# One gather for keys and values, and a GpSimd that weighs them: the edge attention of a four-layer graph network

## The chip, the cores and the metric

The kernel runs on one core of a Trainium2 chip, as one program. The metric is device time in microseconds, the median of three runs. A core has TensorE (PE; PEld is its weight load), VectorE (DVE), ScalarE (ACT), GpSimd (POOL) and SyncE (SP), which only starts DMAs here. Engines run side by side and wait for one another on semaphores. Arithmetic is fp32 throughout.

## What is computed

Four graph layers and four expert layers follow one another on 3125 nodes of 256 features and 50,000 edges sorted by destination. Only the first graph layer matters here:

```python
enh = node_features + 0.1 * query_emb[None, :]        # node_features = layernorm(x)
Q, K, V = [(enh @ W + b).reshape(N, 4, 64) for W, b in ...]
mod_k = K[src] + 0.2 * rel_w[edge_relations][:, None, :]
scores = einsum('ehd,ehd->eh', Q[dst], mod_k) / 64 ** 0.5
ex = exp(scores - segment_max(scores, dst)[dst])
w = ex / segment_sum(ex, dst)[dst]
agg = segment_sum(w[:, :, None] * V[src], dst)
msgs = where(deg > 0, agg, V)
x = layernorm(msgs.reshape(N, 256) @ Wo + bo + node_features) * gamma + beta
```

## The kernel before

The nodes are 25 tiles of 125 (T, P). The edges are 391 chunks of 128. A chunk can touch two node tiles, so the kernel goes through "visits", pairs of a chunk and a tile; there are 416 (VT), done in 104 batches of four (VB). For each visit `tile_of_visit` holds the tile's number, `src_of_visit` the source nodes of the 128 edges, `rel_dst` their destination within the tile.

The phases run one after another, with a barrier of all engines between them:

- `qkv_phase`: VectorE normalises the rows, TensorE turns and multiplies them. A first loop over the tiles makes the keys, in five groups of five tiles (L474 to L505, L532 to L537); a second loop makes values and queries in turn (L538). SP stores each group of keys to the DRAM table `k_table` and of values to `v_table`, 640 KB each (L454). When all keys are stored, GpSimd starts the gathers of the first eight batches (L464).
- `score_phase`: per batch GpSimd gathers the key rows of 4 x 128 edges, 1 KB each, with four indirect DMAs (L93), into a ring of eight batches. VectorE builds 0/1 matrices ("hits", L688), TensorE turns them and multiplies them with queries and relation weights, ScalarE copies, VectorE adds the key rows (L747), multiplies (L751) and reduces (L753). GpSimd refills a slot when L747 has read it (`freed`).
- `weights_phase`: maximum per node by scans, and the exponential. GpSimd meanwhile gathers the value rows of the first eight batches (L860).
- `attend_phase`: GpSimd gathers value rows like the keys. VectorE multiplies them by the weights into `summand` (L1008), copies the weights beside them (L1011), reads the four tile numbers of the batch before from memory into registers (L79), makes the hits three batches ahead (L688), and adds the four products of the batch before, from PSUM, to their tiles of `sums` or `odd_sums` (L997). TensorE multiplies hits and summands (L1034).
- `message_router_phase`: loads the nodes' own values from `v_table` (L1303) and goes on.

No planner decides an order: each engine's queue is the order of the code.

Of the kernel before, what the change touches and what calls it, by code (L numbers as in the profile page):

```python
# [23 lines left out]
N = 3125  # L24
# [60 lines left out]
def early_gathers(env, pool, table):  # L85

    for k in range(RING):
        start_gather(env, pool, table, k)

def start_gather(env, pool, table, k):
    for i in range(VB):
        pool.indirect_dma_start(env.ring[:, k % RING, i, :], None, table, bass.IndirectOffsetOnAxis(  # L93
            env.src_of_visit[:, k * VB + i:k * VB + i + 1], 0)).then_inc(env.gathered[k % RING], 16)

class Gather:

    def __init__(self, env, ph, table, batches):  # L100
        self.env, self.table, self.batches = env, table, batches
        self.rows = env.ring
        self.freed = ph.sem()
        self.passed = ph.sem()
        self.base = list(env.gathered_base)
        for s in range(RING):
            env.gathered_base[s] += 16 * VB * len(range(s, batches, RING))

    def gpsimd(self, pool):
        for k in range(RING, self.batches):  # L110
            pool.wait_ge(self.freed, k - RING + 1)
            pool.sem_inc(self.passed, 1)
            start_gather(self.env, pool, self.table, k)

    def wait(self, engine, k):

        engine.wait_ge(self.env.gathered[k % RING], self.base[k % RING] + 16 * VB * (k // RING + 1))
# [297 lines left out]
def qkv_phase(env):  # L415
# [6 lines left out]
    with ExitStack() as st:  # L422
# [7 lines left out]
        k_rows = sb(env, st, "k_rows", [P, 2 * GT, D])  # L430
        v_rows = sb(env, st, "v_rows", [P, 2 * GT, D])
        turned_ps = ps(env, st, "turned_ps", [128, 2, 512])
        k_ps = ps(env, st, "k_ps", [128, 2, 512])
        q_ps = ps(env, st, "q_ps", [128, 2, 512])
        v_ps = ps(env, st, "v_ps", [128, 2, 512])
        moments = Moments(env, st, ph, "nodes")
        present, prepared, w_landed, bias_landed, query_landed, query_scaled = [ph.sem() for _ in range(6)]
        normed_made, turned, turned_out, k_multiplied, k_made = [ph.sem() for _ in range(5)]
        q_multiplied, v_multiplied, q_made, v_made = [ph.sem() for _ in range(4)]
        k_stored = [ph.sem() for _ in range(2)]  # L440
        v_stored = [ph.sem() for _ in range(2)]
        with nc.Block() as block:

            @block.sync
            def _(sp):
# [4 lines left out]
                for rows, table, made, stored in ((k_rows, env.k_table, k_made, k_stored), (v_rows, env.v_table, v_made, v_stored)):  # L450
                    for g in range(G):
                        half = g % 2
                        sp.wait_ge(made, (g + 1) * GT)
                        sp.dma_start(table[g * GN:(g + 1) * GN, :].rearrange("(t p) d -> p t d", p=P),  # L454
                                     rows[:, half * GT:(half + 1) * GT, :]).then_inc(stored[half], 16)
                for half in range(2):
                    sp.wait_ge(v_stored[half], 16 * len(range(half, G, 2)))

            @block.gpsimd
            def _(pool):  # L460
                pool.memset(eps[:], 1e-5).then_inc(prepared, 1)
                for half in range(2):
                    pool.wait_ge(k_stored[half], 16 * len(range(half, G, 2)))
                early_gathers(env, pool, env.k_table)  # L464

            @block.vector
            def _(v):
# [8 lines left out]
                def keys(g):  # L476
                    if g >= 2:
                        v.wait_ge(k_stored[g % 2], 16 * (g // 2))
                    for t in group(g):
                        v.wait_ge(k_multiplied, t + 1)  # L480
                        v.tensor_tensor(k_rows[:, t % (2 * GT), :], k_ps[0:P, t % 2, 0:D], bias_bc[:, D:2 * D], ALU.add).then_inc(k_made, 1)

                def values(g):
                    if g >= 2:
                        v.wait_ge(v_stored[g % 2], 16 * (g // 2))
                    for t in group(g):
                        v.wait_ge(v_multiplied, t + 1)
                        v.tensor_tensor(v_rows[:, t % (2 * GT), :], v_ps[0:P, t % 2, 0:D], bias_bc[:, 2 * D:3 * D],
                                        ALU.add).then_inc(v_made, 1)
                        v.wait_ge(q_multiplied, t + 1)  # L490
                        v.tensor_tensor(env.q[:, t, :], q_ps[0:P, t % 2, 0:D], bias_bc[:, 0:D], ALU.add).then_inc(q_made, 1)
# [5 lines left out]
                for i in range(G + 1):  # L497
# [6 lines left out]
                    if i >= 1:  # L504
                        keys(i - 1)  # L505
                v.tensor_copy(env.mean[:], moments.mv[:, :, 0:1].rearrange("p t o -> p (t o)"))
                v.tensor_copy(env.rstd[:], moments.rstd[:])
                for g in range(G):
                    values(g)

            @block.tensor
            def _(pe):
                def product(out, t, part, done):
                    for k in range(K2):
                        mm = pe.matmul(out[0:P, t % 2, 0:D], x_t[:, t, k * P:(k + 1) * P], w_sb[:, k, part * D:(part + 1) * D],
                                       start=k == 0, stop=k == K2 - 1)
                    mm.then_inc(done, 1)

                def key(t):
                    pe.wait_ge(turned_out, t + 1)  # L520
                    if t >= 2:
                        pe.wait_ge(k_made, t - 1)
                    product(k_ps, t, 1, k_multiplied)

                pe.wait_ge(w_landed, 16)
                for t in range(T):
# [7 lines left out]
                    if t % GT > 0:  # L534
                        key(t - 1)
                    if t % GT == GT - 1:
                        key(t)  # L537
                for t in range(T):  # L538
                    if t >= 2:
                        pe.wait_ge(v_made, t - 1)  # L540
                    product(v_ps, t, 2, v_multiplied)
# [2859 lines left out]
```

## Time and profile before

| | |
|---|---|
| median of three runs | 5564.5 us (5561.1 to 5566.32) |
| profiled execution | 5557.42 us |
| its span | 5555.6 us |
| TensorE busy | 4191.8 us (75%) |
| VectorE busy | 2496.2 us (45%) |
| GpSimd busy | 2332.9 us (42%) |
| ScalarE busy | 1159.9 us (21%) |
| gathers of keys, L93 | 416, busy 422.5 us |
| gathers of values, L93 | 416, busy 427.6 us |
| DMA over the span | 95 GB/s on average |

The span is the time from the first to the last instruction; the execution's own time lies 1.8 us above it. Busy shares are averages over phases with different limits. "issue" as the reason of an idle stretch means that the engine waited for nothing that the profile shows, mostly for its own sequencer. Each fp32 product of a visit is two records of TensorE (832 for 416).

### The profile page before, as it was taken

What the parts mean: (1) busy time and instruction counts of PE and PEld (TensorE: products, weight loads), DVE (VectorE), ACT (ScalarE), POOL (GpSimd) and SP (SyncE); (2) the same over time, 40 slices, a digit from 0 to 9 for tenths busy, and PEclk for the clock granted to TensorE, in tenths of its full rate; (3) what the DMA queues carried; (4) which work ended last, traced back from release to release, by engine and by line L of the source; (5) the groups of instructions that cost most, each with busy time, mean ns of one, the idle gap of its engine ahead of it and who ended that gap; (6) DMA issues with size and microseconds to landing.
All of it is one profiled execution on the core that took longest, in us unless ns stands there. A gap on an engine that the chain in (4) does not pass through costs nothing. (4 is left out here: it accounts for less than half of the span.)

```text
span 5555.6 us, 68719 instructions
## 1 busy us (share of the span) xinstructions
PE 4191.8 (75%) x20094; PEld 3185.7 (57%) x20094; DVE 2496.2 (45%) x4951; ACT 1159.9 (21%) x2617; POOL 2332.9 (42%) x2376
## 2 busy tenths in 40 slices
PE   5899935554573777799977899766559999665689
PEld 3666623333562555699976888544437677443445
DVE  4799976666525444265656000322223222222253
ACT  1244400000122000232222444200003333100023
POOL 0677767775245777100000111357760000477710
PEclk9999968776696999899987999667889999888888
DMA  2333323331273333210001999333331000233300
GB/s 74 104 101 100 100 71 100 102 102 56 84 229 123 103 103 104 89 39 7 7 31 52 314 322 324 113 88 103 103 102 35 1 1 10 76 102 103 103 24 14
DMA packets 315546, 530.11 MB, mean 95 GB/s; under 512 B 76398, under 2 KB 226171, under 8 KB 315086
## 3 DMA queue, kind: packets, MB, share of 16 engines
q0 software_dynamic: 106944, 292.17, 18.3%
q1 hardware_dynamic: 208268, 233.65, 12.9%
q8 instruction: 189, 3.10, 0.2%
q14 instruction: 145, 1.19, 0.1%
HBM read 471.59 MB, written 54.05 MB: 95 GB/s over the span
## 5 line engine op out<-in xcount | busy, mean ns | idle before, releaser
L2442 POOL DMA_INDIRECT gathered_rows<-k_table,index x1176 | 1153.4, 981 | 1073.5 <-ACT index L2431 716.1
L2528 PE MATMUL sum_ps<-gathered_rows,hit 128*125 (+1 forms) x3328 | 983.9, 451 | 662.6 <-SPq L2448 431.7
L2528 PEld LDWEIGHTS sum_ps<-gathered_rows,hit 128*125 128x125 f32 (+1 forms) x3328 | 704.6, 221 | 941.5 <-issue 825.1
L93 POOL DMA_INDIRECT rows_all<-k_table,src_of_visit x416 | 422.5, 1016 | 197.0 <-issue 118.2
L93 POOL DMA_INDIRECT rows_all<-v_table,src_of_visit x416 | 427.6, 1028 | 147.9 <-issue 126.1
L1034 PE MATMUL ps_sum<-summand,hit 128*125 128x261 f32 x832 | 294.2, 515 | 245.1 <-DVE summand L1011 216.7
L2512 DVE TENSOR_TENSOR node_sums<-node_sums,sum_ps 125x256 f32 x244 | 102.8, 422 | 771.3 <-PE sum_ps L2528 771.3
L1034 PEld LDWEIGHTS ps_sum<-summand,hit 128*125 128x125 f32 x832 | 198.3, 250 | 340.6 <-issue 299.3
L2431 ACT ACTIVATE index<-src_of_chunk 128x4 int32<-128x4 int32 x294 | 59.3, 205 | 1415.1 <-DMA gathered_rows<-k_table,index 1379.7
L1985 DVE TENSOR_TENSOR y<-out_ps,b 128x256 f32<-128x256 f32 x120 | 51.0, 425 | 549.1 <-PE out_ps L1874 549.1
L2736 PE MATMUL qk_ps<-window_sums,composed 128*128 128x126 f32 (+1 forms) x2400 | 291.9, 279 | 0.0
L1833 POOL DMA_INDIRECT rows<-token_table,token_of_slot x120 | 113.5, 946 | 421.7 <-PE turn_ps L1855 408.4
L780 PE MATMUL ps_q<-q,hit_t 125*128 x832 | 286.3, 426 | 0.0
L1874 PE MATMUL out_ps<-w,h 128*128 128x256 f32 x1152 | 272.2, 387 | 17.9 <-ACT h L1934 14.1
L2736 PEld LDWEIGHTS qk_ps<-window_sums,composed 128*128 128x128 f32 x2400 | 276.5, 192 | 8.6
L1865 PE MATMUL hidden_ps<-x_e,w 128*128 128x128 f32 (+1 forms) x2048 | 274.4, 291 | 8.6 <-ACT x_e L1923 7.8
L1865 PEld LDWEIGHTS hidden_ps<-x_e,w 128*128 128x128 f32 x2048 | 261.3, 194 | 19.1 <-ACT x_e L1923 8.2
L2382 ACT ACTIVATE h<-hidden_ps,raw_b,raw_g 128x320 f32<-128x320 f32 (+1 forms) x320 | 195.4, 612 | 336.7 <-PE hidden_ps L2299 336.7
L1934 ACT ACTIVATE h<-hidden_ps,b 128x128 f32<-128x128 f32 (+1 forms) x512 | 194.1, 380 | 314.3 <-PE hidden_ps L1865 288.0
L2512 DVE TENSOR_TENSOR window_sums<-window_sums,sum_ps 126x256 f32 x344 | 144.9, 421 | 247.1 <-PE sum_ps L2528 227.4
L1874 PEld LDWEIGHTS out_ps<-w,h 128*128 128x128 f32 x1152 | 211.6, 190 | 64.1 <-ACT h L1934 38.7
L1557 POOL MEMSET eps<- 125x1 f32 x1 | 0.1, 99 | 588.0 <-POOLq L2683 588.0
(487 smaller groups left out, 7002.6 us busy)
## 6 DMA issues: line engine op xcount, KB each, us to landing
w<-in_L_ffn_W SPq DMA_DIRECT2D x112, 1024.0 KB
gathered_rows<-k_table,index POOLq DMA_INDIRECT x1176, 2.7
w<-in_L_ffn_w SPq DMA_DIRECT2D x64, 256.0 KB, 3.7
b<-in_L_ffn_b SPq DMA_DIRECT2D x88, 128.0 KB, 4.4
y_slots<-y SPq DMA_DIRECT2D x32, 256.0 KB, 4.4
y_slots<-y SPq DMA_DIRECT2D x56, 128.0 KB
rows_all<-k_table,src_of_visit POOLq DMA_INDIRECT x416, 2.8
rows_all<-v_table,src_of_visit POOLq DMA_INDIRECT x416, 2.8
```

Source lines behind the costliest of these rows:

```text
L93: pool.indirect_dma_start(env.ring[:, k % RING, i, :], None, table, bass.IndirectOffsetOnAxis(env.src_of_visit[:, k * VB + i:k * VB + i + ...
L780: pe.matmul(ps_q[:, slot % 2, i, :], hit_t[0:P, slot, i * 128:(i + 1) * 128], env.q[:, ds(tile, 1), :].rearrange("p o d -> p (o d)"), star ...
L1034: mm = pe.matmul(ps_sum[0:P, slot % 2, i, 0:VC], hit[:, slot, i, 0:P], summand[:, slot, i, :], start=True, stop=True)
L1833: pool.indirect_dma_start(rows[:, j % n_slots, c, :], None, env.token_table, bass.IndirectOffsetOnAxis(env.token_of_slot[:, j * cut.tiles ...
L1865: mm = pe.matmul(hidden_ps[:, (s * hc + m) % 4, 0:cut.unit], w1[:, s, k, m * 128:(m + 1) * 128], x_e[:, s % 2, k, :], start=k == 0, stop=k ...
L1874: mm = pe.matmul(out_ps[:, c, 0:D], h[:, s % 2, k, c * 128:(c + 1) * 128], w2[:, s, k, :], start=k == 0, stop=k == hc - 1)
L1934: act.activation(h[:, s % 2, m, :], hidden_ps[:, (s * hc + m) % 4, 0:cut.unit], ACT.Gelu, bias=b1[:, s, m:m + 1]).then_inc(activated, 1)
L2382: act.activation(h[layer][:, m, lo:lo + size], hidden_ps[:, j % ring, 0:size], ACT.Relu, bias=raw[f"b{layer + 1}"][:, col:col + 1], scale= ...
L2442: pool.indirect_dma_start(self.rows[:, (q % SLOTS) * CHUNKS + c, :], None, self.table, bass.IndirectOffsetOnAxis(self.index[:, q % SLOTS, ...
L2512: v.tensor_tensor(here, here, sum_ps[0:rows, k % banks, 0:D], ALU.add).then_inc(summed, 1)
L2528: mm = pe.matmul(sum_ps[0:rows, k % banks, 0:D], hit[:, g % (lead + 1), i * chunks + c, :], gather.rows[:, ds(first[i] + c, 1), :].rearran ...
L2736: mm = pe.matmul(qk_ps[:, n % 2, i * WR:i * WR + nodes], env.composed[:, r, c, m * 128:(m + 1) * 128], s_t[g % 3][:, c, r, 0:nodes], start ...
```

## The change

Keys and values are made together, in products of 512 columns, and stored side by side in one table `kv_table` of 2 KB rows; the second loop makes queries only. The gathers of the score phase bring 2 KB rows, into a ring of four batches (of the same memory). SP stores the value half of each batch in the order of the visits to the DRAM tensor `v_kept`, and GpSimd's next gather into a slot waits for VectorE's reading and for this store. The attend phase has no gathers: SP loads `v_kept` back, one batch per DMA, eight batches deep; GpSimd multiplies by the weights, ScalarE copies the weights, and VectorE makes hits (now four ahead), adds, and then reads the next batch's tile numbers. `sums` is allocated after the weights phase.

```diff
-def start_gather(env, pool, table, k):
+KEPT_RING = 4
+def start_gather(env, pool, k):
     for i in range(VB):
-        pool.indirect_dma_start(env.ring[:, k % RING, i, :], None, table, bass.IndirectOffsetOnAxis(
-            env.src_of_visit[:, k * VB + i:k * VB + i + 1], 0)).then_inc(env.gathered[k % RING], 16)
+        pool.indirect_dma_start(env.ring[:, k % KEPT_RING, i, :], None, env.kv_table, bass.IndirectOffsetOnAxis(
+            env.src_of_visit[:, k * VB + i:k * VB + i + 1], 0)).then_inc(env.gathered[k % KEPT_RING], 16)
...
     def gpsimd(self, pool):
-        for k in range(RING, self.batches):
-            pool.wait_ge(self.freed, k - RING + 1)
+        for k in range(KEPT_RING, self.batches):
+            pool.wait_ge(self.freed, k - KEPT_RING + 1)
+            pool.wait_ge(self.kept[k % KEPT_RING], 16 * (k // KEPT_RING))
             pool.sem_inc(self.passed, 1)
-            start_gather(self.env, pool, self.table, k)
+            start_gather(self.env, pool, k)
+    def sync(self, sp):
+        for k in range(self.batches):
+            self.wait(sp, k)
+            sp.dma_start(self.env.v_kept[k], self.rows[:, k % KEPT_RING, :, D:2 * D]).then_inc(self.kept[k % KEPT_RING], 16)
+        for s in range(KEPT_RING):
+            sp.wait_ge(self.kept[s], 16 * len(range(s, self.batches, KEPT_RING)))
...
@@ qkv_phase
+                for g in range(G):
+                    half = g % 2
+                    sp.wait_ge(kv_made, (g + 1) * GT)
+                    sp.dma_start(env.kv_table[g * GN:(g + 1) * GN, :].rearrange("(t p) d -> p t d", p=P),
+                                 kv_rows[:, half * GT:(half + 1) * GT, :]).then_inc(kv_stored[half], 16)
...
+                        v.tensor_tensor(kv_rows[:, t % (2 * GT), :], kv_ps[0:P, t % 2, :], bias_bc[:, D:3 * D], ALU.add).then_inc(kv_made, 1)
...
+                    product(kv_ps[0:P, t % 2, :], t, slice(D, 3 * D), kv_multiplied)
...
@@ score_phase
+                gather.sync(sp)
...
-                    k_rows = gather.rows[:, k % RING].rearrange("p v (h d) -> p v h d", h=HEADS)
+                    k_rows = gather.rows[:, k % KEPT_RING, :, 0:D].rearrange("p v (h d) -> p v h d", h=HEADS)
...
@@ weights_phase
-                early_gathers(env, pool, env.v_table)
...
@@ attend_phase
+    deep = 8
+        rows = sb(env, st, "v_rows", [128, deep, VB, D])
...
+                for k in range(batches):
+                    if k >= deep:
+                        sp.wait_ge(weighed, k - deep + 1)
+                    sp.dma_start(rows[:, k % deep], env.v_kept[k]).then_inc(landed[k % deep], 16)
...
                 pool.memset(summand[:], 1.0).then_inc(cleared, 1)
-                gather.gpsimd(pool)
+                pool.wait_ge(cleared, 3)
+                for k in range(batches):
+                    slot = k % SLOTS
+                    pool.wait_ge(landed[k % deep], 16 * (k // deep + 1))
+                    if k >= SLOTS:
+                        pool.wait_ge(multiplied, k - SLOTS + 1)
+                    pool.tensor_tensor(summand[:, slot, :, 0:D].rearrange("p v (h d) -> p v h d", h=HEADS),
+                                       rows[:, k % deep].rearrange("p v (h d) -> p v h d", h=HEADS),
+                                       env.scores[:, k * VB:(k + 1) * VB, :].unsqueeze(3).to_broadcast([128, VB, HEADS, HD]),
+                                       ALU.mult).then_inc(weighed, 1)
...
+                for k in range(SLOTS):
+                    hits(k)
+                tiles = tiles_of_batch(v, env.tile_of_visit, 0, T)
+                for k in range(batches):
+                    v.wait_ge(multiplied, k + 1)
+                    if k + SLOTS < batches:
+                        hits(k + SLOTS)
+                    add(k, tiles)
+                    if k + 1 < batches:
+                        tiles = tiles_of_batch(v, env.tile_of_visit, k + 1, T)
...
+            @block.scalar
+                for k in range(batches):
+                    if k >= SLOTS:
+                        act.wait_ge(multiplied, k - SLOTS + 1)
+                    act.activation(summand[:, k % SLOTS, :, D:D + HEADS], env.scores[:, k * VB:(k + 1) * VB, :], ACT.Copy).then_inc(copied, 1)
...
@@ message_router_phase
-                    sp.dma_start(v_own[:, g * GT:(g + 1) * GT, :], env.v_table[g * GN:(g + 1) * GN, :].rearrange(
+                    sp.dma_start(v_own[:, g * GT:(g + 1) * GT, :], env.kv_table[g * GN:(g + 1) * GN, D:2 * D].rearrange(
```

VectorE's queue in the attend phase, one batch from its last addition to the next hits. TENSOR_LOAD and the ISA rows behind it read one tile number. Before:

```order
L997 TENSOR_TENSOR odd_sums<-odd_sums,ps_sum 125x261
L1008 TENSOR_TENSOR summand<-rows_all,scores 128x4x256
L1011 COPY summand<-scores 128x4x4
L79 TENSOR_LOAD tile_of_visit
L79 ISA x2
L79 TENSOR_LOAD tile_of_visit
L79 ISA x2
L79 TENSOR_LOAD tile_of_visit
L79 ISA x2
L79 TENSOR_LOAD tile_of_visit
L79 ISA x2
L688 TENSOR_TENSOR hit<-iota,rel_dst 128x512
```

The same place of the same queue after the change:

```order
L1006 TENSOR_TENSOR odd_sums<-odd_sums,ps_sum 125x261
L79 TENSOR_LOAD tile_of_visit
L79 ISA x2
L79 TENSOR_LOAD tile_of_visit
L79 ISA x2
L79 TENSOR_LOAD tile_of_visit
L79 ISA x2
L79 TENSOR_LOAD tile_of_visit
L79 ISA x2
L683 TENSOR_TENSOR hit<-iota,rel_dst 128x512
```

The multiply and the copy are gone from this queue, and the four loads stand directly behind the fourth addition.

GpSimd's queue from the projections to the attend phase (the branches are the ends of phases). Before:

```order
L93 DMA rows_all<-k_table,src_of_visit 128x256 x32
L442 UNCONDITIONAL_BRANCH
L721 UNCONDITIONAL_BRANCH
L93 DMA rows_all<-k_table,src_of_visit 128x256 x384
L714 UNCONDITIONAL_BRANCH
L858 UNCONDITIONAL_BRANCH
L93 DMA rows_all<-v_table,src_of_visit 128x256 x32
L852 UNCONDITIONAL_BRANCH
L985 UNCONDITIONAL_BRANCH
L987 MEMSET summand 128x4176
L93 DMA rows_all<-v_table,src_of_visit 128x256 x384
```

The same queue after the change:

```order
L96 DMA rows_all<-kv_table,src_of_visit 128x512 x16
L451 UNCONDITIONAL_BRANCH
L717 UNCONDITIONAL_BRANCH
L96 DMA rows_all<-kv_table,src_of_visit 128x512 x400
L709 UNCONDITIONAL_BRANCH
L984 UNCONDITIONAL_BRANCH
L986 MEMSET summand 128x4176
L993 TENSOR_TENSOR summand<-v_rows,scores 128x4x256 x104
```

Sixteen gathers have moved from the projections into the scores, the 416 gathers of values are gone, and 104 multiplies have come.

## Rows read from the trace of the kernel before

**Rows 1.** Stages: stretch, length, busy time of each engine (instructions), clock, DMA share.

```profile
core 0: us, PE busy (x) PEld busy (x) DVE busy (x) ACT busy (x) POOL busy (x), PEclk, DMA share, GB/s
84.00:121.00 37.00, 31.95 (x153) 24.80 (x152) 23.55 (x83) 15.51 (x53) 0.00 (x0) 0.93 0.22 76
121.00:164.00 43.00, 42.65 (x198) 36.75 (x196) 21.25 (x52) 0.00 (x0) 27.35 (x29) 1.00 0.51 159
189.00:700.00 511.00, 502.81 (x2460) 327.34 (x2459) 482.53 (x514) 215.02 (x308) 392.08 (x384) 1.00 0.35 100
776.00:1292.00 516.00, 294.16 (x832) 198.35 (x832) 346.15 (x728) 0.00 (x0) 385.82 (x384) 0.78 0.34 98
```

**Rows 2.** Waits of attend: waiter, releaser, total us, times, longest.

```profile
DVE summand L1008 <- DMA rows_all<-v_table,src_of_visit: 48.4, 79, 1.4
...
POOL rows_all L93 <- issue: 116.7, 383, 0.3
```

**Rows 3.** Timeline of one attend batch: start, us, engine, line, [idle before <-releaser].

```profile
1002.74 1.23 DVE L1008 TENSOR_TENSOR summand<-rows_all,scores 128x1024 f32<-128x1024 f32 x1 [0.18 <-DMA rows_all<-v_table,src_of_visit]
1003.77 1.01 POOL L93 DMA_INDIRECT rows_all<-v_table,src_of_visit  x1 [0.30 <-issue]
1003.88 0.17 DVE L1011 COPY summand<-scores 128x16 f32<-128x16 f32 x1
...
1004.15 3.42 PE L1034 MATMUL ps_sum<-summand,hit 128*125 128x261 f32 x8 [3.06 <-DVE summand L1011]
...
1005.23 0.69 DVE L688 TENSOR_TENSOR hit<-iota,rel_dst 128x512 f32<-128x512 f32 x1 [1.18 <-issue]
...
1006.85 0.42 DVE L997 TENSOR_TENSOR odd_sums<-odd_sums,ps_sum 125x261 f32 x1
```

**Rows 4.** Scores: GpSimd's wait, then forms (times, ns min/median/max, first and last start).

```profile
POOL rows_all L93 <- DVE terms L747: 29.0, 27, 21.1
...
L93 POOL DMA_INDIRECT rows_all<-k_table,src_of_visit x416: 942/946/1998, 128.1 to 696.8; - x139
...
L747 DVE TENSOR_TENSOR terms<-rows_all,ps_rel x104: 1220/1222/1223, 187.1 to 700.5; 128x1024 f32<-128x1024 f32 x104
```

**Rows 5.** Timeline of SP's last key store and GpSimd's first gather inside the scores.

```profile
120.97 0.25 SPq L454 DMA_DIRECT2D k_table<-k_rows  x1
...
189.12 1.29 POOL L93 DMA_INDIRECT rows_all<-k_table,src_of_visit  x1 [21.11 <-DVE terms L747]
```

**Rows 6.** GpSimd's arithmetic in the message stage: forms, timeline, and a one-element memset.

```profile
L1328 POOL TENSOR_TENSOR own<-own,bias_bc x25: 721/727/1949, 1313.9 to 1369.0; 125x256 f32<-125x256 f32 x25
...
L1325 POOL TENSOR_SCALAR own<-x,mean,rstd x25: 1215/1221/1895, 1312.6 to 1367.3; 125x256 f32<-125x256 f32 x25
...
1328.17 1.73 DVE L1351 TENSOR_TENSOR msg<-sums,rden 125x256 f32<-125x256 f32 x5
...
1328.53 1.95 POOL L1328 TENSOR_TENSOR own<-own,bias_bc 125x256 f32<-125x256 f32 x1
...
L461 POOL MEMSET eps<- 125x1 f32 x1 | 0.1, 98 | 74.2 <-POOLq L204 74.2
```

**Rows 7.** DMA: gather queue in the scores, SP's queue overall, a stage of large loads.

```profile
q0 software_dynamic: 18427, 50.36, 34.5%
...
q1 hardware_dynamic: 208268, 233.65, 12.9%
...
3100.00:3200.00 100.00, 96.90 (x648) 88.55 (x647) 5.53 (x13) 46.85 (x130) 11.59 (x13) 1.00 1.01 330
```

**Rows 8.** Timeline: end of the weights stage, first hits and last addition of attend.

```profile
747.05 3.59 DVE L958 COPY scores<-score_ps 128x512 f32<-128x512 f32 x4 [0.46 <-PE score_ps L885]
...
755.66 0.95 POOL L93 DMA_INDIRECT rows_all<-v_table,src_of_visit  x1 [0.30 <-issue]
...
773.92 1.90 DVE L688 TENSOR_TENSOR hit<-iota,rel_dst 128x512 f32<-128x512 f32 x3
...
1291.84 0.42 DVE L997 TENSOR_TENSOR odd_sums<-odd_sums,ps_sum 125x261 f32 x1
```

More of the change, by code:

```diff
@@ L449, in _ @@
                 sp.dma_start(bias_bc[:], env.row("qkv_b").to_broadcast([P, 3 * D])).then_inc(bias_landed, 16)
[L450 to L455, printed above, removed]
+                for g in range(G):
[3 more added lines that the diff above has]
+                                 kv_rows[:, half * GT:(half + 1) * GT, :]).then_inc(kv_stored[half], 16)
                 for half in range(2):
-                    sp.wait_ge(v_stored[half], 16 * len(range(half, G, 2)))
+                    sp.wait_ge(kv_stored[half], 16 * len(range(half, G, 2)))
             @block.gpsimd
@@ L504, in _, with product, key_value @@
                     if i >= 1:
[L505 removed]
+                        keys_values(i - 1)
                 v.tensor_copy(env.mean[:], moments.mv[:, :, 0:1].rearrange("p t o -> p (t o)"))
                 v.tensor_copy(env.rstd[:], moments.rstd[:])
[L508 to L509 removed]
+                for t in range(T):
+                    v.wait_ge(q_multiplied, t + 1)
+                    v.tensor_tensor(env.q[:, t, :], q_ps[0:P, t % 2, 0:D], bias_bc[:, 0:D], ALU.add).then_inc(q_made, 1)
             @block.tensor
             def _(pe):
[L513 removed]
+                def product(out, t, columns, done):
                     for k in range(K2):
[L515 to L516 removed]
+                        mm = pe.matmul(out, x_t[:, t, k * P:(k + 1) * P], w_sb[:, k, columns], start=k == 0, stop=k == K2 - 1)
                     mm.then_inc(done, 1)
[L519 removed]
+                def key_value(t):
                     pe.wait_ge(turned_out, t + 1)
                     if t >= 2:
[L522 to L523 removed]
+                        pe.wait_ge(kv_made, t - 1)
+                    product(kv_ps[0:P, t % 2, :], t, slice(D, 3 * D), kv_multiplied)
                 pe.wait_ge(w_landed, 16)
@@ L700, in score_phase @@
         rel_w = sb(env, st, "rel_w", [R64, HD])
-        gather = Gather(env, ph, env.k_table, batches)
+        gather = Gather(env, ph, batches)
         hit = sb(env, st, "hit", [128, SLOTS, VB, 128])
@@ L977, in attend_phase @@
         ps_sum = ps(env, st, "ps_sum", [128, 2, VB, 512])
-        cleared, hits_made, multiplied, summed = [ph.sem() for _ in range(4)]
+        cleared, hits_made, multiplied, summed, weighed, copied = [ph.sem() for _ in range(6)]
+        landed = [ph.sem() for _ in range(deep)]
         with nc.Block() as block:
@@ L1001, in _ @@
                 v.wait_ge(cleared, 3)
-                v.sem_inc(summed, VB)
-                for k in range(AHEAD):
-                    make_hits(v, env, hit[:, k], env.rel_dst, 128, k).then_inc(hits_made, 1)
-                def one_batch(k, slot, lap):
-                    gather.wait(v, k)
-                    v.tensor_tensor(summand[:, slot, :, 0:D].rearrange("p v (h d) -> p v h d", h=HEADS),
-                                    gather.rows[:, k % RING].rearrange("p v (h d) -> p v h d", h=HEADS),
-                                    env.scores[:, ds(k * VB, VB), :].unsqueeze(3).to_broadcast([128, VB, HEADS, HD]), ALU.mult)
-                    v.tensor_copy(summand[:, slot, :, D:D + HEADS], env.scores[:, ds(k * VB, VB), :]).then_inc(gather.freed, 1)
-                    before = not isinstance(k, int) or k > 0
-                    if before:
-                        tiles = tiles_of_batch(v, env.tile_of_visit, k - 1, T)
-                        v.wait_ge(multiplied, k)
-                    make_hits(v, env, hit[:, (slot + AHEAD) % SLOTS], env.rel_dst, 128, k + AHEAD).then_inc(hits_made, 1)
-                    if before:
-                        add(k - 1, (slot + SLOTS - 1) % SLOTS, tiles)
@@ L1026, in _ @@
             @block.tensor
             def _(pe):
-                def one_batch(k, slot, lap):
+                for k in range(batches):
+                    slot = k % SLOTS
                     pe.wait_ge(hits_made, k + 1)
-                    pe.wait_ge(gather.freed, k + 1)
-                    if not isinstance(k, int) or k >= 2:
-                        pe.wait_ge(summed, (k - 1) * VB + VB)
+                    pe.wait_ge(weighed, k + 1)
+                    pe.wait_ge(copied, k + 1)
+                    if k >= 2:
+                        pe.wait_ge(summed, (k - 1) * VB)
@@ L3339, in build @@
             weights_phase(env)
+            env.sums = sb(env, l0, "sums", [P, T, VC])
             attend_phase(env)
```

88 lines of the change are left out of this document (35 added, 53 removed).

## The prediction

> **What bounds the kernel now.** I read the table of stages first [rows 1]. The change touches five stretches of one program on one core: the projections (84 to 164 us), the scores (189 to 700), the softmax weights (to 757), the weighted sums or "attend" stage (776 to 1292), and the first loads of the message stage. Everything from 1300 on keeps its instructions, so I carry it over unchanged. Scores and attend are about 515 us each, and each has 104 batches, so a batch costs 4.9 to 5.0 us in both. In the scores TensorE is busy 98%, VectorE 94% and GpSimd's gathers fill the rest of its time. In attend nothing looks full: TensorE 57%, VectorE 67%.
>
> Then I read who waits for whom [rows 2]. In attend GpSimd waits almost only for "issue": 383 gaps of 0.3 us, one behind each gather. VectorE waits 79 times for a gather to land, 48 us in all. So the chain is gather, multiply, matmul, and it is the gather issue that paces it. The close-up shows it [rows 3]: a gather of 1.01 us and its gap of 0.3 make 1.31, one of 0.95 makes 1.25, four to a batch, hence 5.0 to 5.2 us. VectorE's own batch is multiply from 1002.74 to 1003.88, copy, four tile numbers, hits at 1005.23, four additions ending at 1007.27: 4.5 us of work in a 5.1 us period.
>
> The scores are nearly tied [rows 4]. GpSimd waited for VectorE's first reading 29.0 us in 27 waits, and 21.1 of them is the start at 189.12 [rows 5]. The ring of eight batches was filled before the stage; GpSimd lost that lead slowly. 384 gathers took 189.1 to 696.8+0.95, less 7.9 us of those waits: 1.302 us each, 5.21 us a batch. VectorE alone would need (700.5-187.1)/103 = 4.98.
>
> **Attend.** Removed: 384 gathers here and 32 in the weights stage, VectorE's 104 multiplies (1.23 us) and 104 copies (0.17). Added: 104 loads of 512 KB by SP, 104 multiplies of 128x1024 on GpSimd, 104 tiny copies on ScalarE, which is otherwise idle.
>
> The new price is GpSimd's multiply. No row has that size. The nearest is a two-input add of 125x256 at 0.727 us median over 25 [rows 6]. A one-element GpSimd memset costs 0.10, so four times the row less three fixed parts is 2.61 us; without that deduction 2.91. The scores are read with a repeated element, which no row has; the upper bound is the tensor-scalar row, 1.221 us for 256, which makes 4.6. I take 2.61 to 2.7, since the operation is the same as in the first row.
>
> It doesn't run alone. At 1328.53 the same add took 1.95 us while VectorE ran five operations with two SBUF inputs from 1328.17 to 1329.90; it ended 0.58 after them [rows 6]. So GpSimd stands still while VectorE reads two SBUF tensors. In the new batch VectorE has one such instruction left, the hits of 0.69 us; the additions read one of their inputs from PSUM. Each multiply thus loses up to 0.69: 2.65+0.69 = 3.34.
> The Trainium skill ("SBUF — State Buffer", section "SBUF: two separate sides") calls the port pair that the two engines share an exclusive lock for a whole instruction, between a VectorE operation with two SBUF inputs and a GpSimd one that reads SBUF. By that rule 3.34 is the floor and the hits can also wait up to one whole multiply; without it the floor would be VectorE's 2.97 below. The row at 1328.53 agrees with the rule.
>
> VectorE's new batch: hits and four additions, 1005.23 to 1007.27 = 2.04 us, then four tile numbers. They took 1003.88 to 1005.23 = 1.35 us, of which only the 0.17 copy ran beside them [rows 3]; VectorE's sequencer starts them when the last instruction before them starts. Behind the fourth addition 0.42 is hidden and 0.93 shows: 2.97 us a batch. So moving them saves only 0.2 to 0.4 us; the queue shows that they stand between the fourth addition and the next hits, as before between the copy and the hits.
>
> TensorE needs 3.42 us for a batch's eight passes at 1004.15 [rows 3]; the granted clock of this stage is 0.78 [rows 1], so it moves between 1.2 and 2.4 GHz, and 3.42 is the slow case, half of it the fast one. It works two PSUM slots ahead of the additions. At 3.4 us a batch it just fits even at 1.2 GHz.
>
> The new wait of GpSimd is for the load and for the matmul four batches back. Loads: 512 KB each 3.4 us is 154 GB/s, against 330 GB/s at a full DMA share [rows 7], eight batches deep. Hidden. SP has nothing else in the stage. ScalarE's copy costs the path nothing: its inputs are ready before the stage and it waits only for the slot. The message stage loads its values in the same 1 KB pieces from every second kilobyte; I cost that at nothing.
>
> So three engines need 3.34, 2.97 and 1.7 to 3.4. I take 3.4 a batch, bounds 3.0 (VectorE paces, no exclusion) and 3.9 (2.91 plus 0.69 plus waits). From the first hits at 773.92 to the last addition's end at 1292.26 are 518 us [rows 8]; new: 2.6 for the first multiply, 104 x 3.4 = 354, 3.4 for the last matmuls and additions: 360. **Minus 158.**
>
> **Weights.** VectorE's last copies end at 747.05+3.59 = 750.6, but GpSimd's early gathers of values end at 755.66+0.95 = 756.6 and hold the stage [rows 8]. They go. **Minus 6.** Next late is VectorE itself.
>
> **Projections and the start of the scores.** The same 150 products of 256 columns are computed, as 50 of 512 and 50 of 256; a pass of 256 columns takes 0.22 us (43 us for 198 [rows 1]), and one of 512 I take as two. But now values are made in the first loop: 25 tiles x 0.86 us more there, and as much less in the second. VectorE's bias additions of 512 instead of 256 columns stay under TensorE's pace in both. The first loop had slack (32.0 of 37 us busy, VectorE 23.6 [rows 1]); after it TensorE fills it: 25 x 2.15 us (four passes of 512, two transposes of 0.22) and 1 us a group make 59 us instead of 37, the second 22 instead of 43. The end of the queries moves by about +2. What matters is the table: the last key store was issued at 120.97 and gathers began at 128.1 [rows 4, 5]. Now the last store is issued near 144.5, and is twice as big: 7.1 us grow to about 12. Gathers from 156.5, sixteen x 1.25 = 20, end 177 instead of 168.0 (189.12 less its idle 21.11). **Plus 9** at the start of the scores.
>
> **Scores.** GpSimd must now issue 400 gathers inside the stage instead of 384, because the ring holds four batches: 400 x 1.302 = 521 us from 198, and the last batch lands at 722; before 700.55. That is +21.6, of which 9 are the start's, so **plus 12.6** here. The 7.9 us of waits are gone, since GpSimd can no longer run ahead; VectorE, 4.98 a batch, waits for it. The row is twice as long, but a gather still has 128 of them; I take the same 0.946 us, the lower bound, and hold an unseen surcharge of up to 0.1 in the range (+40).
> The DMA engines: gathers alone are 34.5% of 16 engines [rows 7], 1.80 us of each 5.21. Twice the bytes cost between 1.80 (a price per descriptor) and 3.60 (per byte). Stores of values, 512 KB a batch, at q1's rate (233.65 MB in 12.9% of 5555.6 us, 326 GB/s) cost 1.61. Sum 3.4 to 5.2 of 5.21 us: from two thirds to full. I take 4.9 and **plus 8** for late landings. A slot of the ring lives: 5.2 issue, 3.5 landing, about 5 store, 14 of the 20.8 us that four slots give. SP's store queues behind nothing but older stores; behind GpSimd's new wait stand only the next gathers.
> The Trainium skill ("DMA: Bandwidth & Descriptors", section "Issuing engines are not separate DMA queues") says that DMAs of all queues run on the same 16 engines and interleave. By it the store isn't free though SP is idle; the projections show it, where both kinds ran at once with a share of 0.51 at 159 GB/s [rows 1].
>
> **Sum**: -158 -6 +9 +12.6 +8 = -134. The profiled execution is 5557.4 us, so 5423; the median of the runs is 7 above it: **5430**.
>
> **Rivals.**
> *VectorE paces attend* (15%). If the two engines share SBUF without loss, 2.97 a batch: 104 x 0.43 = 45 less, 5385. For it: the gather at 1003.77, begun beside VectorE's multiply of two SBUF tensors, is stretched by 0.06 only [rows 3]. Against: 1.95 at 1328.53.
> *The DMA engines or the four slots pace the scores* (17%). At 5.2 us of DMA work in 5.21, queues grow; 5.7 a batch instead of 5.29 makes +43, 5475. For it: the per-byte sum. Against: longer rows carry less overhead, and 330 GB/s has been seen at full share.
> *GpSimd's multiply is slow* (7%), slower than before. At the tensor-scalar row's rate it takes 4.6, with the hits 5.3: attend 557 us, +39, and with +30 and -6 elsewhere 5627. It decides from 4.69 us a batch (3.4 + 134/104), that is a multiply over 4.0 us. For it: a repeated operand. Against: the same class of operation at 0.727.
> *The tile numbers aren't hidden at all* (3%): 2.04+1.35 = 3.39 on VectorE, which ties with the forecast; with the two out of step 3.8, 5470.
>
> **Numbers.** Forecast 58%. The low end is 2.97 a batch and no crowding, 5370; the high end takes 3.8 a batch (+42) and +33 more in the scores, 5505. Left out are the slow multiply and the tails. A kernel within 0.2% (11 us) can't be told from no change here: 2%. Faster 90%, slower 8%.
>
> **What would show it.** Right: GpSimd's multiplies 2.6 to 3.4 us long with the stretched ones beside the hits; attend 350 to 365 us; a gap of about 0.9 us before each hits on VectorE; score stage with DMA share 0.85 to 1.0, GpSimd waiting for neither stores nor VectorE, and VectorE idle 0.2 to 0.4 us a batch for a landing. Wrong: gathers over 1.0 us on median in the scores, GpSimd waiting there for the stores, or attend under 320 or over 410 us.

## The result and the profile after

The changed kernel takes 5506.6 us (5503.6 to 5508.8) against 5564.5 before, both medians of four runs: ratio 0.9896, 95% interval [0.9884, 0.9909]. It is faster by 58 us, where 134 were forecast, and 1.6 us beyond the high end of the range. The profiled span is 5507.0 us (before 5555.6).

The experiments below were measured in five sets of runs, each beside the kernel before; ratios are taken within a set, because in sets one, three and four every kernel took longer (the kernel before 6077.1, 6111.3 and 6072.3 us, against 5558.7 and 5557.2 in sets two and five), and one of the four runs of *tiles_between_f*, 13244.8 us at a granted clock of 0.49, is left out of its figures.

Where the time went, from landmarks of the two traces: the first gather inside the scores is 3.2 us later (192.35 against 189.12; forecast +9); the last key reading starts at 742.9 instead of 700.5, so the scores add 39.1 (forecast 12.6 and 8); the weights give 7.0 back (forecast 6); the stretch between them and the first hits of attend 3.3; attend gives 88.7 (forecast 158). At attend's end the kernel is 56.5 us ahead, at the end of the program 48.6; the 8 between arise after 5389 us, in the last stage, whose instructions are the same.

The stages after, as in [rows 1]:

```profile
core 0: us, PE busy (x) PEld busy (x) DVE busy (x) ACT busy (x) POOL busy (x), PEclk, DMA share, GB/s
84.00:164.00 80.00, 73.51 (x249) 42.28 (x247) 40.74 (x106) 15.55 (x53) 9.72 (x11) 0.97 0.32 112
192.00:735.00 543.00, 517.02 (x2434) 332.75 (x2434) 475.44 (x507) 212.86 (x305) 420.04 (x399) 0.97 0.90 287
806.00:1236.00 430.00, 259.71 (x832) 176.14 (x832) 222.85 (x522) 22.35 (x104) 213.24 (x104) 0.84 0.37 118
```

In attend every engine is idle for 40% of the time or more, GpSimd for half of it. The waits say who holds whom (waiter, releaser, us, times, longest), beside [rows 2]:

```profile
POOL summand L993 <- PE ps_sum L1045: 198.3, 98, 5.8
DVE hit L683 <- issue: 191.1, 96, 2.3
PE ps_sum L1045 <- DVE odd_sums L1006: 162.3, 101, 4.1
```

GpSimd waits for TensorE, TensorE for VectorE's additions, and VectorE for nothing shown: 2 us of "issue" ahead of nearly every hits. One batch, beside [rows 3]:

```profile
1003.00 0.69 DVE L683 TENSOR_TENSOR hit<-iota,rel_dst 128x512 f32<-128x512 f32 x1 [1.97 <-issue]
...
1003.33 2.12 POOL L993 TENSOR_TENSOR summand<-v_rows,scores 128x1024 f32<-128x1024 f32 x1 [1.88 <-PE ps_sum L1045]
...
1004.62 0.42 DVE L1006 TENSOR_TENSOR odd_sums<-odd_sums,ps_sum 125x261 f32 x1
...
1007.35 0.69 DVE L683 TENSOR_TENSOR hit<-iota,rel_dst 128x512 f32<-128x512 f32 x1 [2.31 <-issue]
```

```profile
L79 DVEq TENSOR_LOAD <-tile_of_visit x416: 296/299/553, 806.1 to 1233.5; - x139
L79 DVEq FUSED_REGOPS  x416: 183/186/211, 806.7 to 1233.8; - x139
L79 DVEq SEQ_ASSERT  x416: 23/23/35, 806.9 to 1234.0; - x139
...
L79 DVEq TENSOR_LOAD <-tile_of_visit x1: 308/308/308, 1004.5 to 1004.5; - x1
...
L79 DVEq TENSOR_LOAD <-tile_of_visit x1: 297/297/297, 1006.1 to 1006.1; - x1
L79 DVEq TENSOR_LOAD <-tile_of_visit x1: 298/298/298, 1006.7 to 1006.7; - x1
```

A read is 0.30 + 0.19 + 0.02 = 0.51 us and the next starts 0.6 after it. Four make 2.4 us, and all but the first 0.4 of them stand alone: the gap ahead of the hits is 1.97 us in the median (here 2.31). The kernel before has the same reads, and in the batch of [rows 3] they start at

```profile
L79 DVEq TENSOR_LOAD <-tile_of_visit x1: 316/316/316, 1002.8 to 1002.8; - x1
L79 DVEq TENSOR_LOAD <-tile_of_visit x1: 298/298/298, 1003.4 to 1003.4; - x1
...
L79 DVEq TENSOR_LOAD <-tile_of_visit x1: 297/297/297, 1004.6 to 1004.6; - x1
```

that is with the multiply (1002.74), not with the copy behind it (1003.88). The prediction's 1.35 us were the time from the copy's start to the hits: the 0.17 copy and the 1.18 us of the reads that stuck out behind it. The other 1.2 us of the reads lay beneath the multiply and the copy.

In the scores, beside [rows 4] and, for the queues, [rows 7] (the gathers' first and last start, then waits, then TensorE's queue):

```profile
L96 POOL DMA_INDIRECT rows_all<-kv_table,src_of_visit x400: 942/947/1995, 192.4 to 735.5; - x134
...
DVE terms L743 <- PE ps_rel L778: 55.7, 80, 3.9
POOL rows_all L96 <- DVE terms L743: 28.4, 20, 21.2
PEld ps_q L776 <- issue: 37.4, 75, 1.1
PE ps_q L776 <- issue: 20.6, 49, 0.9
POOL rows_all L96 <- DMA v_kept<-rows_all: 8.5, 28, 0.3
DVE terms L743 <- DMA rows_all<-kv_table,src_of_visit: 1.4, 1, 1.4
...
L775 PEldq TENSOR_LOAD <-tile_of_visit x416: 294/301/1459, 181.5 to 740.4; - x139
```

VectorE hardly waits for a landing (1.4 us), but 56 us for TensorE (before 9.8); and TensorE has gaps of "issue" ahead of its query products, 37 us at their weight loads (before 1.2). The gathers' median is as before, yet 400 of them take 544 us, 1.36 each (before 384 in 509, 1.32). With GpSimd's waits for VectorE and the stores taken off, as in the prediction's 1.302, it is 1.32.

### The profile page after: what moved, and what is told of

Its sections match the earlier page's. It is cut to its first block and busy times, and to the rows that moved or that the text cites. A ratio compares the mean times of both kernels' runs of the same rounds, so it can differ in the third digit from the quotient of the medians.

```text
span 5507.0 us, 68392 instructions
## 1 busy us (share of the span) xinstructions
PE 4188.6 (76%) x19994; PEld 3157.8 (57%) x19994; DVE 2366.0 (43%) x4715; ACT 1183.2 (21%) x2721; POOL 2134.7 (39%) x2064
## 5 line engine op out<-in xcount | busy, mean ns | idle before, releaser
L96 POOL DMA_INDIRECT rows_all<-kv_table,src_of_visit x416 | 436.6, 1049 | 221.9 <-issue 111.8
L1045 PE MATMUL ps_sum<-summand,hit 128*125 128x261 f32 x832 | 259.7, 465 | 180.6 <-DVE odd_sums L1006 162.3
L1045 PEld LDWEIGHTS ps_sum<-summand,hit 128*125 128x125 f32 x832 | 176.1, 222 | 264.1 <-issue 232.3
L776 PE MATMUL ps_q<-q,hit_t 125*128 x832 | 294.8, 437 | 22.4 <-issue 20.6
L993 POOL TENSOR_TENSOR summand<-v_rows,scores 128x1024 f32<-128x1024 f32 x104 | 213.2, 2052 | 208.5 <-PE ps_sum L1045 198.3
L683 DVE TENSOR_TENSOR hit<-iota,rel_dst 128x512 f32<-128x512 f32 x210 | 155.4, 741 | 202.8 <-issue 191.1
```

Source lines behind the costliest of these rows:

```text
L96: pool.indirect_dma_start(env.ring[:, k % KEPT_RING, i, :], None, env.kv_table, bass.IndirectOffsetOnAxis(env.src_of_visit[:, k * VB + i:k ...
L776: pe.matmul(ps_q[:, slot % 2, i, :], hit_t[0:P, slot, i * 128:(i + 1) * 128], env.q[:, ds(tile, 1), :].rearrange("p o d -> p (o d)"), star ...
L993: pool.tensor_tensor(summand[:, slot, :, 0:D].rearrange("p v (h d) -> p v h d", h=HEADS), rows[:, k % deep].rearrange("p v (h d) -> p v h ...
L1045: mm = pe.matmul(ps_sum[0:P, k % 2, i, 0:VC], hit[:, slot, i, 0:P], summand[:, slot, i, :], start=True, stop=True)
```

## The experiments

Of sets one, three and four only attend of the changed kernels is read in microseconds: with the reads between the additions it takes 3.19 to 3.20 us a batch in all four runs, while the scores of that kernel last 665 us in *tiles_between* and 554 in *tiles_between_f*.

**Attend: what are the 2 us?** Theory A says the four reads, theory B GpSimd or the port that it shares with VectorE. Set one (before 6077.1 us).

*tiles_once* reads the numbers once, for all batches (so it computes other sums):

```
                     add(k, tiles)
-                    if k + 1 < batches:
-                        tiles = tiles_of_batch(v, env.tile_of_visit, k + 1, T)
```

> The changed kernel, but attend reads four tile numbers once, before its loop, and uses them for all batches (so all additions go to the same four tiles: part of the computation is changed). Theory A, the tile numbers pace attend: VectorE's batch of 4.00 us is 2.03 us of hits and additions and 1.97 us of four reads that nothing covers. Without them the next limit shows, GpSimd's 2.1 plus 0.7 us of hits or TensorE's 2.0 to 3.8: 2.8 to 3.4 us a batch, attend 295 to 355 us instead of 430, total 5390 to 5440. Theory B, GpSimd and the shared port pace it (multiply, matmul, slot wait): the batch stays at 3.8 to 4.0 us, total over 5485.

5685.6 us, 0.9358 [0.9342, 0.9374]. Its multiplies, then VectorE's hits beside one:

```profile
L993 POOL TENSOR_TENSOR summand<-v_rows,scores x104: 2342/2346/2400, 906.4 to 1144.2; 128x1024 f32<-128x1024 f32 x104
...
1001.08 4.65 POOL L993 TENSOR_TENSOR summand<-v_rows,scores 128x1024 f32<-128x1024 f32 x2
...
1002.93 1.04 DVE L683 TENSOR_TENSOR hit<-iota,rel_dst 128x512 f32<-128x512 f32 x1
```

(1144.2 - 906.4)/103 = 2.31 us a batch, under the 2.8 to 3.4 expected: without the reads GpSimd paces, back to back.

*tiles_between* keeps the result and reads one number of the next batch ahead of each addition:

```
                     for i in range(VB):
+                        if k + 1 < batches:
+                            ahead.append(v.value_load(env.tile_of_visit[0:1, ds((k + 1) * VB + i, 1)], min_val=0, max_val=T - 1))
                         if k * VB + i >= 2:
...
-                    if k + 1 < batches:
-                        tiles = tiles_of_batch(v, env.tile_of_visit, k + 1, T)
+                    tiles = ahead
```

> The changed kernel, but the next batch's tile numbers are read one by one ahead of each of the four additions, so that the first is read while the hits run. Same result. Theory A: four reads of 0.5 to 0.6 us one behind the other, with everything else of VectorE beside them but a part of the hits: 2.6 to 3.2 us, and with GpSimd and TensorE as next limits 2.9 to 3.5 a batch; attend 300 to 365 us, total 5400 to 5445. Theory B: no change, 5506.

5778.0 us, 0.9502 [0.9482, 0.9523]; attend (1247.5 - 918.6)/103 = 3.19 us a batch.

*weigh_on_vector* takes GpSimd's multiply back to VectorE, ahead of the reads:

```
+                def weigh(k):
+                    slot = k % SLOTS
+                    v.wait_ge(landed[k % deep], 16 * (k // deep + 1))
+                    v.tensor_tensor(summand[:, slot, :, 0:D]..., rows[:, k % deep]..., scores..., ALU.mult).then_inc(weighed, 1)
```

> The changed kernel, but VectorE weighs the values again (multiply two batches ahead, behind the additions and ahead of the tile numbers); loads of the kept values, ScalarE's copies and the score phase stay. Theory A: the 1.2 us multiply runs beside the four reads, as in the kernel before the change, so the batch is 4.0 to 4.3 us and attend 425 to 450 us: moving the multiply to GpSimd was worth 0 to 0.2 us a batch, total 5505 to 5530. Theory B, the multiply was real work on the path: 4.0 + 1.2 = 5.2 a batch, total 5620 to 5635.

5861.2 us, 0.9651 [0.9625, 0.9678]; attend (1333.9 - 915.2)/103 = 4.07 us a batch, against 4.01 in *no_value_store*, whose attend differs from the changed kernel's only in where it loads from. Moving 1.22 us off VectorE was worth 0.06 us at most: the multiply had been the reads' cover.

**Scores: where do 39 us come from?** C: the stores of values crowd the DMA engines. D: the 2 KB rows or the four slots. *no_value_store* leaves out the stores and the wait for them; attend loads as many bytes from `kv_table` (other sums):

```
-            pool.wait_ge(self.kept[k % KEPT_RING], 16 * (k // KEPT_RING))
...
-                gather.sync(sp)
```

> The changed kernel without the stores of values in the scores and without GpSimd's wait for them; attend loads the same number of bytes from the table instead (so wrong values are summed). Scores took 552.6 us from first to last reading of keys, 5.37 a batch, gathers 1.049 us on mean, against 1.016 before. Theory C, the stores crowd the gathers (DMA share 0.90): the gather's mean returns to 1.02 and the stage to about 530 us, total 5480 to 5490. Theory D, the longer rows or the ring of four cost it: the stage stays over 545 us and the total within 5 us of 5506.

5868.7 us, 0.9655 [0.9636, 0.9673], in set one, whose scores aren't read: it settles nothing. Repeated in set two (before 5558.7), with three others:

> The changed kernel without the 104 stores of values in the scores and without GpSimd's wait for them; attend loads rows of the key-value table of the same size and pattern instead, so the result is another. The gathers still bring 2 KB rows into four slots. Theory C (the stores crowd the gathers on the DMA engines): the score stage shrinks from 543 us to 515 to 525, the mean gather goes back from 1.049 to about 1.02 us, and TensorE's gaps for tile numbers in the scores go from 58 us to a few. Theory D (the long rows and the four slots cost it, not the stores): the stage shrinks by under 8 us and the gathers keep 1.048, as they did in the disturbed run of this kernel.

> The changed kernel as it is, run beside the next three so that they can be compared on one chip. Expected: 0.99 of the kernel before, scores about 5.37 us a batch and attend about 4.0, if this chip does not disturb the scores as the one of the first four runs did.

*ring5* is the changed kernel with `KEPT_RING = 5`; *before_ring4* the kernel before with `RING = 4`:

> The changed kernel with five slots of four gathers instead of four. Four more gathers are issued ahead of the stage, 4 x 1.36 = 5.4 us fewer in it. If a slot comes free too late with four (28.4 us of GpSimd's waits for VectorE, 8.5 for stores), those waits shrink: scores shorter by 5 and up to 20 us. If gather issue and the DMA engines pace the stage, only the 5.4 us less those that the projections get longer, so the total within 5 us of the changed kernel.

> The kernel before with a ring of four batches instead of eight, keys and values still gathered apart in 1 KB rows. It has the changed kernel's slots without its long rows and stores. If the ring is what costs: 16 more gathers in each of the two stages (16 x 1.30 = 20.8 us, of which the scores had 7.9 in hand), so scores +13 and attend up to +21, and more if slots come free late: 1.004 to 1.01 of the kernel before. If the ring alone is harmless (gathers issued ahead were only moved), the total within 0.3%. In both cases the mean gather stays at 1.016 us; were it 1.05 here too, neither rows nor stores would be its cause.

The changed kernel (*after_again*) takes 5515.8 us (0.9923 [0.9903, 0.9942]); without stores 5516.5 (0.9922 [0.9906, 0.9939]); five slots 5521.9 (0.9936 [0.992, 0.9953]); before with four slots 5601.8 (1.0073 [1.0056, 1.009]). Against the changed kernel neither the stores' absence nor a fifth slot moves the total. In the profiled runs the scores, from first to last reading of keys, last 564.4, 558.1 (without stores) and 553.7 us (five slots), but 552.6 in the changed kernel's first run: two runs of one kernel differ by more than these edits. Four slots alone cost the kernel before 43 us; its scores last 536.6 us instead of 513.4. So 23 us of the growth of 39 (51 in *after_again*) come with the ring, where the sum had 12.6; rows and stores together are the rest, and no run parts them cleanly.

What the stores do is in TensorE's queue: its tile-number reads, without stores, and before with four slots:

```profile
L773 PEldq TENSOR_LOAD <-tile_of_visit x416: 294/298/497, 183.0 to 746.6; - x139
```
```profile
L779 PEldq TENSOR_LOAD <-tile_of_visit x416: 293/299/495, 176.6 to 715.7; - x139
```

Never over 0.50 us, against 1.46 after. Of the 416 loads of the changed kernel 98 take over 0.6 us, 73 us above 0.30 each in sum (1.2 us without stores). Those that start 1.0 to 2.5 us behind the issue of a 512 KB store last 0.92 us on average, those over 4 us behind it 0.30:

```profile
L775 PEldq TENSOR_LOAD <-tile_of_visit x1: 1217/1217/1217, 408.7 to 408.7; - x1
...
407.18 3.56 SPq L124 DMA_DIRECT2D v_kept<-rows_all  x2
```

Why nothing is won without them is in the waits of *no_value_store_b* (its gathers, then VectorE's releasers at the key addition):

```profile
L96 POOL DMA_INDIRECT rows_all<-kv_table,src_of_visit x416: 942/946/2001, 152.7 to 745.5; - x139
...
  DMA rows_all<-kv_table,src_of_visit: 48.4, 52
  PE ps_rel L776: 23.5, 24
```

VectorE now waits 48 us for landings and 24 for TensorE, and the gathers inside the stage average 1.075 us. The long ones have one thing in common. Nearly every gather that starts in the first 1.0 us of VectorE's multiply by the queries (`terms<-terms,q_rows`, two inputs in SBUF) ends only 0.78 us after the next instruction, the reduction, has begun; all 90 gathers over 1.0 us in *after_again* end there. Here, 401.18 + 0.79 = 400.33 + 1.64:

```profile
399.93 1.22 DVE L745 TENSOR_TENSOR terms<-terms,q_rows 128x1024 f32<-128x1024 f32 x1
...
400.33 1.64 POOL L96 DMA_INDIRECT rows_all<-kv_table,src_of_visit  x1 [0.30 <-issue]
...
401.18 1.22 DVE L747 TENSOR_REDUCE scores<-terms 128x16 f32<-128x1024 f32 x1
```

Over the stage these gathers take 28.9 us more than 0.946 each before, 32.1 with four slots, 42.8 and 57.4 in the two runs of the changed kernel, 51.6 without stores.

**Theory E: these stretches set the scores.** *q_from_psum* multiplies straight from PSUM, without ScalarE's copy, same result; *both* adds the reads between the additions; *before_tiles_once* is the kernel before with its reads done once (other sums). Set three (before 6111.3):

```
-                    v.wait_ge(q_copied, k + (1 + SLOTS))
-                    v.tensor_tensor(terms[:], terms[:], q_rows[:, slot], ALU.mult).then_inc(summed, 1)
+                    v.tensor_tensor(terms[:], terms[:], ps_q[:, slot % 2], ALU.mult).then_inc(summed, 1)
```

> The changed kernel, with the same result, whose multiply by the queries reads them from PSUM itself, without ScalarE's copy into SBUF; its time on VectorE should stay near 1.22 us, as that of the key addition, which reads PSUM too. Theory E: of the changed kernel's gathers those that start within 1.0 us of the start of this multiply, then an instruction with two SBUF inputs, end only 0.78 us after the next instruction (the reduction) has begun, and take up to 1.99 us instead of 0.946; 57.4 us were lost so in the run beside the last three, 42.8 in the first one, 28.9 in the kernel before. By it no gather of the scores takes more than about 0.96 us now, the mean falls from 1.05 to 1.09 to 0.95, and the 400 gathers take 500 us: the stage from 192 ends near 695 instead of 735 to 749, the total 5506 less 40 to 50, about 5460. Theory C or D (stores or long rows slow the gathers themselves): the mean stays over 1.03 and the stage within 10 us of the changed kernel.

> The changed kernel with each tile number of the next batch read ahead of an addition of this one, same result; here on a chip that does not disturb the scores. Theory A (the four reads behind the last addition pace attend): attend falls from 4.0 to about 3.2 us a batch as on the other chip, 104 x 0.8 = 83 us, total about 5425. Theory B (GpSimd, the port or TensorE pace it): within 20 us of the changed kernel.

> The last two edits together, same result. They act in two stages, so their gains should add: 5506 less 80 less 45, about 5380, which would be the fastest of all. If the gain of one depends on the clock or on what the other leaves, less.

> The kernel before, whose attend reads the four tile numbers once and uses them for every batch, so that the sums are other ones. It asks what these reads cost there. Theory A': nothing, within 0.3% of the kernel before, because GpSimd's gathers pace attend at 5.0 us a batch and most of the reads run beside the multiply of 1.22 us that stands ahead of them. If they were on the path there as in the changed kernel, attend would shrink by up to 104 x 1.35 = 140 us.

Ratios 0.9684 [0.9663, 0.9705], 0.9497 [0.9479, 0.9515], 0.9554 [0.9538, 0.9571] and 0.9922 [0.9903, 0.9941]. Set four (before 6072.3) repeated all four: 0.9729, 0.9504, 0.9574 and 0.9955 [0.994, 0.997]. The gains don't add: in both sets *both* takes 38 us longer than *tiles_between* alone, where it should have been the fastest of all, and no run shows why. The kernel before gains 28 and 46 us when the reads go, neither nothing nor 140; whether it does where it takes 5560 us wasn't measured. Set five (before 5557.2):

> The changed kernel with the tile numbers read between the additions, the last look. Theory A: attend 3.2 us a batch; where the kernel before takes about 5560 us, the total is about 5425, 0.975 of it; where it takes about 6080, 0.950 as three times before.

> The changed kernel with the queries multiplied straight from PSUM, the last look. Where the kernel before takes about 5560 us: theory E gives a stage of the scores that ends near 695 to 705 and a total of 5460 to 5475; if TensorE and VectorE pace the stage it stays at 5500 to 5515. Where it takes about 6080: 0.968 to 0.973 as twice before.

*tiles_between_f*: 5417.0 us, 0.9749 [0.9729, 0.9768], the fastest kernel that computes the same result. Its attend (the window's columns as in [rows 1]):

```profile
L993 POOL TENSOR_TENSOR summand<-v_rows,scores x104: 1897/1901/2398, 805.8 to 1134.1; 128x1024 f32<-128x1024 f32 x104
...
815.00:1149.00 334.00, 204.28 (x816) 144.77 (x816) 299.69 (x516) 21.38 (x98) 190.93 (x101) 1.00 0.46 147
```

3.19 us a batch, VectorE busy for 90% of it, TensorE's clock now 1.00 (2.4 GHz) instead of 0.84 in the mean.

*q_from_psum_f*: 5504.6 us, 0.9904 [0.9888, 0.9921], the changed kernel's time. Theory E holds for the gathers and falls for the time:

```profile
L96 POOL DMA_INDIRECT rows_all<-kv_table,src_of_visit x416: 940/946/1368, 151.3 to 728.5; - x139
...
L742 DVE TENSOR_TENSOR terms<-rows_all,ps_rel x104: 1214/1222/1223, 190.5 to 743.3; 128x1024 f32<-128x1024 f32 x104
...
  PE ps_rel L775: 67.6, 60
```

No gather over 1.37 us, and GpSimd is done 7 us sooner, but the last key reading starts at 743.3, as in the changed kernel: VectorE waits 68 us for TensorE, whose loads are still held up (94 of 416 over 0.4 us, the longest 1.79). The reading that fits these runs is that two limits lie side by side: gathers stretched beside a multiply of two SBUF tensors, and TensorE's loads beside the stores. Taking one away leaves the other: without stores the first sets the pace, with PSUM queries the second. Both at once was not tried, so this stays argued.

## Why the prediction was wrong

- **Direction, removed work, weights**: right. The gathers of values and 7.0 us of the weights went (forecast 6), attend got shorter, no wait of attend ends on a load of values. The low end of the range doesn't add up: 2.97 a batch (-45) and no crowding (-8) make 5377, not 5370.
- **Attend, VectorE's term. This step failed**: "They took 1003.88 to 1005.23 = 1.35 us, of which only the 0.17 copy ran beside them", hence 0.93 us shown and 2.97 a batch. I took the gap between two executed instructions for the length of the reads, and "VectorE's sequencer starts them when the last instruction before them starts" is not what the kernel before shows: they began at 1002.8, with the multiply ahead of that copy. The rows of the queue show 2.4 us of reads. The change took the multiply's cover away and left 0.42 of an addition: 2.04 + 1.97 = 4.0 us a batch, on VectorE. (4.0 - 3.4) x 104 = 62 of the 69 us missing in attend. The rival "aren't hidden at all" named the right engine, with the same wrong 1.35, and got 3%. In *tiles_between_f* the place of the reads alone gives (4.0 - 3.19) x 104 = 84 us back.
- **Attend, GpSimd's term**: 2.65 + 0.69 = 3.34 was too high as well, by its sizes; beside the right reads it would not have paced either. The multiply takes 1.90 us alone and 2.35 back to back with hits (tiles_once). The form held: the two take turns. Hits (0.69 us alone) that begin during a multiply end 0.55 us after it (1001.63 + 1.75 against 1000.93 + 1.90, and 1005.08 + 1.39 against 1004.01 + 1.90, below), so a batch costs GpSimd 1.90 and about 0.4. The Trainium skill ("SBUF — State Buffer", section "SBUF: two separate sides") calls the port pair an exclusive lock, and these rows of *tiles_between_f* agree:

```profile
1000.93 1.90 POOL L993 TENSOR_TENSOR summand<-v_rows,scores 128x1024 f32<-128x1024 f32 x1 [1.43 <-PE ps_sum L1047]
...
1001.63 1.75 DVE L683 TENSOR_TENSOR hit<-iota,rel_dst 128x512 f32<-128x512 f32 x1
...
1004.01 1.90 POOL L993 TENSOR_TENSOR summand<-v_rows,scores 128x1024 f32<-128x1024 f32 x1 [1.18 <-PE ps_sum L1047]
...
1005.08 1.39 DVE L683 TENSOR_TENSOR hit<-iota,rel_dst 128x512 f32<-128x512 f32 x1
```

- **TensorE's 3.42**: not a limit. Its eight passes took 2.0 us in the median and up to 3.82, and it waited for the additions.
- **Projections**: the first gather started 11.8 us after the last store's issue, as forecast (12), but that store was issued at 139.4, not 144.5; the sixteen gathers ended at 171.1, not 177, and 3.2 of 9 arrived.
- **Scores**: 39.1 against 20.6. The 400 gathers in place of 384 were right in kind and too small (12.6, against 23 in *before_ring4*). "Plus 8 for late landings" had the smaller wait: VectorE lost 1.4 us to landings in the first run and 17 in *after_again*, but 56 and 51 to TensorE; the median gather stayed at 0.947 us, as forecast, and the mean grew by gathers begun beside the multiply. Whether the longer rows have a part in that isn't shown. Attend's 69 us and these 18.5 make 88, the last stage gives 8 away, and the start (6), the weights (1), the stretch to the first hits (3) and the step from the profiled runs to the medians (9) give back 19: the 76.5 between forecast and result.

## What to carry to other kernels

Reads of numbers from SBUF into registers are instructions of the engine's queue, and in these profiles they show only in its rows. Before moving work off an engine, look at what its queue does beneath that work: the longest instruction may be the cover of the reads, and then moving it is worth nothing (here 0.06 us of 1.22). What helped here was to spread the reads, one ahead of each addition. And when taking away a suspected cost moves nothing, look for a second limit of the same size before calling the cost harmless.

## What the runs showed of the hardware

- A tile number read from SBUF takes VectorE's queue 0.30 + 0.19 + 0.02 us, 0.6 from one to the next, and TensorE's 0.30 + 0.15 + 0.02 (*after*). With 512 KB stores from SBUF in flight TensorE's load grows from 0.30 to up to 1.46 us (*after*) and 1.79 (*q_from_psum_f*); without them none took over 0.50.
- A 128x1024 multiply with a repeated operand takes GpSimd 1.90 us (*tiles_between_f*), against 1.22 on VectorE (*weigh_on_vector*); in turns with one 128x512 hits instruction of VectorE a batch it takes 2.35 (*tiles_once*).
- Issuing a gather of 128 rows takes GpSimd 0.946 us in the median with 1 KB rows (*before*) as with 2 KB (*no_value_store_b*). Begun beside VectorE's multiply of two SBUF tensors it takes up to 2.0; with one of the two in PSUM the longest took 1.37 (*q_from_psum_f*).
